# Attention of a fused layer: the transposes and copies of two score tiles made together, behind every second tile

## The reference

```python
def _L0_attn_ref(x, Wq, Wkv, null_kv, Wout):      # x: 2 x 1024 x 128, float32
    q = (x @ Wq).reshape(b, n, 16, 64).transpose(0, 2, 1, 3) * 64 ** -0.5
    kv = x @ Wkv                                   # one 64-wide head of keys = values
    kv = jnp.concatenate([null_kv broadcast, kv], axis=1)        # 1025 keys
    sim = jnp.einsum('bhid,bjd->bhij', q, kv)      # causal mask, then softmax
    out = jnp.einsum('bhij,bjd->bhid', softmax(sim), kv)
    return out.transpose(0, 2, 1, 3).reshape(b, n, 1024) @ Wout
```

## Time and profile before

| | |
|---|---|
| median of 3 runs | 1385.38 us (1384.53 to 1386.17) |
| the profiled execution's own time | 1378.48 us |
| its span in the trace | 1376.8 us |
| the attention in it | about 398 to 983 us |
| PE, DVE, ACT, POOL busy over the span | 91%, 81%, 66%, 22% |
| one pair of heads in mid-stage (605.38 to 639.44) | 34.06 us: PE busy 32.93, DVE 24.53, ACT 18.70, POOL 12.01 |

### The profile page before, as it was taken

One profiled execution on the slowest core, in us unless ns is written; L12 is line 12 of the kernel. 1 busy time (PEld: TensorE's weight loads), 2 busy tenths in 40 slices (PEclk: granted clock), 3 DMA queues, 4 the chain that ended last, 5 costly groups with the idle time before them and its releaser, 6 DMA issues. The chain is left out here.

```text
span 1376.8 us, 30320 instructions
## 1 busy us (share of the span) xinstructions
PE 1254.1 (91%) x9584; PEld 519.6 (38%) x9584; DVE 1116.7 (81%) x1937; ACT 907.9 (66%) x1879; POOL 296.6 (22%) x520
## 2 busy tenths in 40 slices
PE   4599999999979999999989999999868999999996
PEld 2122222222245555555565555555642222222222
DVE  6899999999886777777745777776669999999997
ACT  3189999998845555555533555555325999998894
POOL 4300000002003333333312333333223000000200
PEclk9699999999989999999999999999977999999998
DMA  4612122453110000000000000000053212235422
GB/s 109 206 45 55 52 62 66 93 81 78 32 35 18 18 19 18 17 18 18 19 18 18 19 19 17 17 16 1 1 138 105 64 52 55 56 80 97 78 55 62
DMA packets 53789, 69.74 MB, mean 51 GB/s; under 512 B 21264, under 2 KB 31440, under 8 KB 53712
## 3 DMA queue, kind: packets, MB, share of 16 engines
q1 hardware_dynamic: 53712, 68.75, 20.3%
HBM read 37.79 MB, written 22.54 MB: 44 GB/s over the span
## 5 line engine op out<-in xcount | busy, mean ns | idle before, releaser
L920 DVE TENSOR_REDUCE neg_max<-ps 128x1 f32<-128x1024 f32 x512 | 591.4, 1215 | 23.4 <-PE ps L1194 21.3
L756 ACT ACTIVATE arena<-ps 128x512 f32<-128x512 f32 x1024 | 545.4, 597 | 83.0 <-PE ps L1209 70.8
L1209 PE MATMUL ps<-arena 50*128 50x512 bf16 x1024 | 322.9, 387 | 15.4 <-ACT arena L756 10.1
L1225 PE MATMUL ps<-arena 128*32 128x256 f32 (+1 forms) x3584 | 315.8, 424 | 8.6 <-ACT arena L756 3.1
L992 DVE TENSOR_REDUCE a_neg_max<-ps 128x1 f32<-128x129 f32 (+7 forms) x256 | 193.6, 756 | 149.6 <-PE ps L1332 146.6
L1194 PE MATMUL ps<-arena 48*128 48x512 bf16 x1024 | 297.3, 396 | 15.0 <-DVE neg_max L920 14.0
L591 POOL TENSOR_SCALAR arena<-arena,a_rsum 128x128 f32<-128x128 f32 (+7 forms) x256 | 192.2, 751 | 413.3 <-DVE a_rsum L998 413.0
L676 ACT ACTIVATE arena<-ps,a_neg_max 128x129 f32<-128x129 f32 (+7 forms) x256 | 189.8, 741 | 76.6 <-DVE a_neg_max L992 76.2
L684 ACT ACTIVATE arena<-ps 128x128 f32<-128x128 f32 (+1 forms) x192 | 87.3, 454 | 198.5 <-PE ps L1345 197.8
L1326 PE MATMUL ps<-arena 64*128 64x321 f32 (+7 forms) x512 | 194.2, 458 | 12.8 <-ACT arena L676 10.3
L1328 PE MATMUL ps<-arena 64*128 64x128 f32 (+6 forms) x512 | 197.8, 467 | 0.0
(11 more groups left out here) (117 smaller groups left out, 839.1 us busy)
## 6 DMA issues: line engine op xcount, KB each, us to landing
arena<-stack_dram SPq DMA_DIRECT2D x128, 192.0 KB, 3.4
stack_dram<-arena SPq DMA_DIRECT2D x48, 256.0 KB, 3.9
o_dram<-arena SPq DMA_DIRECT2D x32, 256.0 KB, 2.1
arena<-arena SPq DMA_DIRECT2D x32, 256.0 KB, 3.4
arena<-o_dram SPq DMA_DIRECT2D x30, 256.0 KB, 4.2
arena<-max_dram SPq DMA_DIRECT2D x256, 1.0 KB
x<-in_L_attn_x SPq DMA_DIRECT2D x2, 512.0 KB, 4.6
max_dram<-max_T SPq DMA_DIRECT2D x64, 8.0 KB, 1.6
```

The lines of the kernel that those rows point to most:

```text
L756: nc.scalar.activation(probs[:, t, :], ps[:, EXP_BANK[t], :], ACT.Exp, scale=F_SCALE).then_inc(probs_ready, 1)
L920: nc.vector.tensor_reduce(neg_max[:, g, t:t + 1], ps[:, bank:bank + 2, :].rearrange("p a b -> p (a b)"), AX, ALU.max, negate=True).then_in ...
L1209: ins = nc.tensor.matmul(ps[:, bank, :], stack[rows, g, 1, kt * P:(kt + 1) * P], stack[rows, g, 0, h * HALF:(h + 1) * HALF], start=True, s ...
L1225: ins = nc.tensor.matmul(ps[row:row + 32, PV_BANK, cols], v_unit[:, g, t // 2, :], probs[:, t, cols], start=j == 0 and c0 == 0 and g % 2 == 0,
```

## The change

In the three engine programs the same rule is put in place of the old one. Odd steps take the transposes (PE) and the copies (DVE, ACT) of tiles t - 5 and t - 4, one after the other, where each step took those of tile t - 4. Even steps have none. Nothing is added or removed: each pair still has 72 block transposes and 24 copies. The waits inside `a_transposes` and `a_evac` are the same.

```diff
@@ scalar engine, attention body
-                            if t >= A_LAG:
-                                a_evac(pg, t - A_LAG)
-                            elif not (first and k == 0):
-                                a_evac(pg - 1, NS + t - A_LAG)
+                            for s in ((t - A_LAG - 1, t - A_LAG) if t % 2 else ()):
+                                if s >= 0:
+                                    a_evac(pg, s)
+                                elif not (first and k == 0):
+                                    a_evac(pg - 1, NS + s)
@@ vector engine, attention body, behind a_maximum(pg, t): the same lines
@@ tensor engine, attention body, behind a_score_tile(pg, b, k, t, no_q)
-                            if t >= A_LAG:
-                                a_transposes(pg, t - A_LAG)
-                            elif not (first and k == 0):
-                                a_transposes(pg - 1, NS + t - A_LAG)
+                            for s in ((t - A_LAG - 1, t - A_LAG) if t % 2 else ()):
+                                if s >= 0:
+                                    a_transposes(pg, s)
+                                elif not (first and k == 0):
+                                    a_transposes(pg - 1, NS + s)
```

## The result

| | median | range of the runs |
|---|---|---|
| before | 1385.51 us (4 runs) | 1384.53 to 1386.17 |
| after | 1458.20 us (4 runs) | 1455.44 to 1459.77 |

What follows compares the result with a forecast made beforehand. PE was taken to bound the attention; 16 pairs at 3.04 - 0.07 us and 15 at 1.66 made 72.4 us more, 1450.9 profiled, scaled to a median of 1458 us. The range for 8 in 10 was 1432 to 1482.

Steps and rivals of the forecast that it cites:

- The bound: In the attention PE is the bound, busy for 32.93 of 34.06 us in a mid-stage pair; its busy time stays.
- Bank wait, step 13: Second tile's transposes wait for DVE's maximum (769 keys), then its copy of the shared bank: stall 1.38 us.
- Step 15: Second tile's transposes wait for DVE's maximum of 1025 keys, then the bank's copy: stall 1.42 us.
- Step 1: Maximum is short, so the bank's own round counts, transposes of successive tiles 1.50 us apart: stall 0.95 us.
- Step 3: DVE is late from step 2, so maximum 3 and the bank's copy come late: stall 1.44 us.
- Score tile 11: Waits for the exponentials of tile 9 with less PE work between: old 0.47 us becomes 0.70.
- Old pauses: Three PE pauses at the large tiles, 0.73, 0.47 and 0.35 us, go with the old order: minus 1.55 per pair.
- Score tile 15: New wait of 0.36 us: ACT holds the copy of tile 9's last two blocks ahead of tile 13's exponentials.
- Changeovers: Seven transposes-to-64-row-tile changes per pair vanish, a mask precedes such tiles instead, 0.15 us taken: -0.07 us per pair.
- Only the bank's own round: Rival: four stalls of 3.36 us together, no score tile waits; +28 us, 1414; chance 0.07.
- The delays feed each other: Rival: late ACT copies hold exponentials, score tiles, maxima and next copies; +2.0 us per pair, 1490; chance 0.10.
- The clock falls: Rival: long transpose runs with pauses halve PE's clock for 5 us of each pair's work; +80 us, 1539; chance 0.03.

Runs made afterwards that it cites:

- e5: Changed kernel with DVE's copy of the first tile ahead of the maximum in steps 13, 15, 1 and 3 only; 1431.41 us, ratio to before 1.0360.
- e8: Changed kernel with uses reversed: DVE copies each large tile's short group, ACT the four blocks; 1445.11 us, ratio to before 1.0451.
- e1: Changed kernel with the step's score tile between the two tiles' transposes on PE, and the maximum between the copies on DVE; 1409.58 us, ratio to before 1.0178.
- e3: Changed kernel with only tiles 8 to 15 (steps 12 to 3) taken in twos, small ones one per step; 1459.25 us, ratio to before 1.0554.
- e2: Changed kernel with only tiles 0 to 7 (steps 4 to 11) taken in twos, large ones one per step; 1391.43 us, ratio to before 1.0054.
- e10: Changed kernel with ACT making the odd step's exponentials before it copies tile t - 4; 1459.82 us, ratio to before 1.0556.
- e4: Changed kernel with DVE's copy of tile t - 5 ahead of the maximum in all odd steps; 1447.00 us, ratio to before 1.0447.
- e9: Changed kernel with half of the values (step 1) and a query projection (step 3) between the two tiles' transposes on PE; 1443.02 us, ratio to before 1.0427.

## Why the prediction was right, step by step

- **The bound.** PE bounds the attention; its waits turned into time. The growth of shown idle, 66.6 us, and the 0.17 us that each of 32 new waits of transposes doesn't show (5.4 us) make 72.0 us. The medians differ by 72.7; the forecast's sum was 72.4. That the two agree within 1 us is closer than the measurement can tell, and some of it is luck, as below.
- **Bank wait, step 13.** Forecast 1.38, measured 1.26 in the loop and 1.35 outside. Mis-sized was the way from the copy's end to PE: 0.15 taken, 0.05 measured in the loop, 0.15 outside.
- **Step 15.** Forecast 1.42, measured 1.48 and 1.40. **Step 1.** 0.95 against 0.84 and 0.93. **Step 3.** 1.44 against 1.51 to 1.65 and 1.41. The sum is 5.1 to 5.2 where 5.19 was forecast. That the maximum ahead of the copy and the copy's length make the stall is shown by e5 and e8; that neighbours on a shared bank do, by e1 and e3, where the tiles of one use, in e2, cost a tenth of it.
- **Score tile 11.** Forecast 0.70, 0.23 more than before. Measured 0.70 outside the loop (658.04 to 658.90, less the 0.16 of a changeover) and 0.89 in it, where the kernel before has 0.47 and 0.65: 0.23 and 0.24 more.
- **Old pauses.** 1.55 was read from one stretch across the end of the loop. The kernel before has 0.64 + 0.65 + 0.58 = 1.87 in the loop and 0.52 + 0.47 + 0.35 = 1.34 outside, and eight pairs of each: 1.60 on average. That the stretch taken lies near it is luck.
- **Score tile 15.** In the loop the prediction's picture failed, though the number held: forecast as a term of its own, 0.36, measured 0.31. e10 took the wait away and the stretch stayed as long, so there it is no cost of its own: DVE's chain from tile 9's copy to tile 10's sets the stretch, and the wait and the stall of step 15 share it (0.31 + 1.48 = 1.79, forecast 0.36 + 1.42 = 1.78). The prediction started step 15 from its mask with DVE free. In the loop DVE was not free: maximum 15 starts at 630.69, 0.44 behind its mask rather than 0.27, which adds 0.17; the copy's way to PE, 0.05 rather than 0.15, takes 0.10 off again. Outside the loop the picture holds: maximum 15 starts 0.27 behind its mask, the stall is 1.40, and e10 won 0.25 us there.
- **Changeovers.** From a mask to a 64-row matmul 0.15 was taken as the middle of two ends; measured 0.16 (639.90 to 640.06, from the mask of step 2 to score tile 3).
- **Rivals.** "Only the bank's own round" would be 1414. Its four stalls, 3.36 us, are close to e5's 3.20, once the maximum is out of the way; but e5 takes 1431, as the score tiles' waits, which this rival put at nothing, are still there (0.32 at score tile 15, 0.70 and 0.88 at score tile 11). "The delays feed each other" would have shown more waits for exponentials than 33; it is what e4 made happen. "The clock falls": in the changed kernel the granted clock was 1.00 from 414 to 1048 us, through runs of 15 transposes with a pause in the middle, but for some 3 us at 0.50 from 746 on, in the output product between the batches (the kernel before has none there). In e10, with a longer pause in step 15, it fell behind four pairs, as said. The Trainium skill ("TensorE: Matmul & The Clock Gate", PE-mode transpose) says that transposes don't engage the full clock. The changed kernel's transposes run 0.11 us apart at 1.00, so as it stands this isn't borne out. Whether transposes or the pauses between them made e10's clock fall, no run separates.

## What to carry to other kernels

Before two producers are put next to each other, look at which of them share a buffer: the second waits for the first one's consumer, and for all that stands ahead of that consumer in its engine's queue, so the price is the maximum plus the copy and not the copy alone. Give the short copy to the engine whose queue holds the long operations, and put work that needs no such buffer between two users of it; but follow who comes next, since an operation that moves up pushes something back (e4 and e9 lost a half and a third of what they won). Two waits in a row on one engine can be one chain on another: take one away and see if the distance over both shrinks. Look at each kind of pair for it, and at the clock: the time alone would have said that e10 changed nothing.

## What the runs showed that I had not expected

- The pairs in the loop and those written out around it have the same work and differ in small things: PE goes on 0.05 us behind the copy's end in the loop and 0.15 outside, and score tile 11 waits 0.89 and 0.70. It decides whether the wait of score tile 15 costs anything. I have no experiment on the reason.
- An order that only moved a wait (e10) brought stretches at half clock that the changed kernel's pairs don't have.
- Costs of parts are not additive here: 0.5% for the small tiles and 5.5% for the large ones give 5.4% together, since each order has another score tile wait.
